# Attention with routed experts on one core: the boundary between early and late tokens moved from 48 to 52 of 64 tiles

## What is computed

```python
x = x + tanh(g_xattn[0]) * attention(layernorm(x), ctx, ctx, Wq, Wk, Wv, Wp, bp)   # 16 heads of 8
x = x + tanh(g_ffn[0]) * experts(layernorm(x), gate, w0, w1, wo)

# experts: 8 of them, hidden size 256, each token goes to two
top_k_weights, top_k_indices = top_k(x @ gate, 2)
p = softmax(top_k_weights)
y = sum over the two chosen n of  p[n] * ((silu(x @ w0[n]) * (x @ w1[n])) @ wo[n])
```

## Time and profile before

| | |
|---|---|
| median of 3 runs | 582.92 us (582.74 to 583.54) |
| the profiled execution, its own time | 583.09 us |
| its span in the trace | 581.3 us |
| outside the span | 1.8 us |
| mean granted TensorE clock | 0.983 |

### The profile page before, as it was taken

The page is one execution under the profiler, slowest core; times in us unless marked ns, Lnnn a source line. Parts: engine busy times, 40 slices in busy tenths (PEclk is TensorE's granted clock), DMA queues, the critical chain, the costliest instruction groups (busy, mean ns, idle before and its releaser), DMA issues.

```text
span 581.3 us, 20236 instructions
## 1 busy us (share of the span) xinstructions
PE 548.9 (94%) x5964; PEld 459.1 (79%) x5965; DVE 405.7 (70%) x1356; ACT 411.7 (71%) x1083; POOL 379.2 (65%) x520
## 2 busy tenths in 40 slices
PE   8999999999999999999999998799999999999960
PEld 6777777777777777777777777699999999999950
DVE  5888988898888888898898875634333333335773
ACT  4788888888888888888898887456566666655640
POOL 3236676767767767767676657777767666766770
PEclk9999999999999999999999999989999999999995
DMA  3742121121221211212212113333323333336997
GB/s 86 219 132 73 49 83 57 53 74 55 61 66 59 77 50 59 77 50 74 67 53 79 40 49 107 133 102 107 104 91 95 91 91 95 94 91 182 324 322 217
DMA packets 70246, 57.96 MB, mean 100 GB/s; under 512 B 8966, under 2 KB 66062, under 8 KB 70192
## 3 DMA queue, kind: packets, MB, share of 16 engines
q1 hardware_dynamic: 52672, 35.98, 21.6%
q0 software_dynamic: 8640, 16.93, 8.7%
q10 hardware_dynamic: 8880, 4.39, 2.6%
HBM read 29.84 MB, written 24.15 MB: 93 GB/s over the span
## 4 chain that ended last, share of the span: by engine, by line
PE 80%; issue 7%; DVE 6%; POOL 3%; DMA 2%; ACT 1%; POOLq 0%; SPq 0%; ACTq 0%; DVEq 0%
PE psH L546 18%; PE psH L460 12%; PE psO L516 8%; PE psH L446 7%; PE psH L452 6%; PE psK L494 5%; PE psO L560 5%; PE psG L560 4%; PE psO L487 3%; PE psO L488 3%; PE psO L476 2%; DVE mx L872 2%; POOL results L1132 2%; PE psX L468 2%; PE psX L498 1%
## 5 line engine op out<-in xcount | busy, mean ns | idle before, releaser
L1132 POOL DMA_INDIRECT results<-ys,zin x142 | 142.0, 1000 | 54.8 <-issue 50.3
L1083 POOL DMA_INDIRECT lists<-zp,dest x128 | 128.2, 1002 | 63.5 <-DVE dest L887 33.6
L546 PE MATMUL psH<-zT,wcur 128*128 128x256 f32 x568 | 135.9, 383 | 0.0
L625 ACT ACTIVATE ex<-psH,rs 128x512 f32<-128x512 f32 x128 | 81.1, 684 | 51.8 <-PE psH L452 51.8
L546 PEld LDWEIGHTS psH<-zT,wcur 128*128 128x128 f32 x568 | 103.3, 192 | 11.3
L992 DVE TENSOR_TENSOR hm<-psH,hs 128x512 f32<-128x512 f32 x71 | 49.1, 692 | 85.9 <-PE psH L546 51.2
L872 DVE TENSOR_REDUCE mx<-psH 128x8 fp32r<-128x512 f32 x128 | 82.5, 686 | 5.0 <-PE psH L446 0.3
L516 PEld LDWEIGHTS psO<-v,pT 128*64 128x64 f32 x2048 | 64.9, 138 | 24.9 <-ACT v L671 23.1
L1114 POOL TENSOR_TENSOR kvr<-ropA,ropB 128x256 f32<-128x256 f32 x64 | 46.5, 727 | 50.4 <-DVE ropB L949 50.0
L460 PE MATMUL psH<-ident,ex 128*128 128x128 f32 x512 | 76.3, 284 | 0.3 <-ACT ex L625 0.2
L516 PE MATMUL psO<-v,pT 128*64 128x64 f32 x2048 | 73.7, 225 | 0.4 <-DVE x1r L940 0.4
(11 more groups left out here) (157 smaller groups left out, 991.5 us busy)
## 6 DMA issues: line engine op xcount, KB each, us to landing
zin<-lists SPq DMA_DIRECT2D x71, 130.0 KB, 2.1
yy<-results SPq DMA_DIRECT2D x16, 512.0 KB, 5.5
xres<-x1r SPq DMA_DIRECT2D x32, 128.0 KB, 2.2
out_dram<-xres ACTq DMA_DIRECT2D x16, 256.0 KB, 4.1
xring<-in_x_dram SPq DMA_DIRECT2D x31, 128.0 KB
cring<-in_ctx_dram SPq DMA_DIRECT2D x31, 128.0 KB
results<-ys,zin POOLq DMA_INDIRECT x142, 2.3
lists<-pad SPq DMA_DIRECT2D x16, 130.0 KB, 2.8
```

Source lines behind the costliest of these rows:

```text
L546: last = pe.matmul(bank[t.buf(2)][:, k * ET:(k + 1) * ET], wcur[:, t.buf(2), a, k * P:(k + 1) * P], zT[:, t.buf(2), :], start=True, stop=True)
L625: nc.scalar.activation(ex[:, t.buf(2), h, :].rearrange("p (g c) -> p g c", g=2), psH[h][:, :, 0:256], ACT.Exp, scale=rs[:, t.buf(4) // 2, ...
L1083: nc.gpsimd.indirect_dma_start(lists, bass.IndirectOffsetOnAxis(ap=dest[:, t.buf(4), j:j + 1], axis=0), zp[:, t.buf(4), j, :], None).then_ ...
L1132: nc.gpsimd.indirect_dma_start(results, bass.IndirectOffsetOnAxis(ap=zin[:, t.buf(8), h, D:D + 1].bitcast(U32), axis=0), ys[:, t.buf(8), h ...
```

## The change

`EARLY` becomes 52 in place of 48. By the formulas of the code `NFULL` becomes 45 in place of 41, `NEARLY` 59 in place of 55 and `CHUNKS_EARLY` 13 in place of 12. `COMBINE_AT` was 60 and is now `NEARLY + 5` = 64. A new constant `CHUNKS_INSIDE` = 72 − 64 = 8 counts the chunks that are summed inside the steps; it was 12 under the old formula. Chunks 8 to 12 are early, but are summed after the last step.

```diff
-EARLY = 3 * NT // 4
+EARLY = 13 * NT // 16
...
-COMBINE_AT = NET + 1 - CHUNKS_EARLY
+COMBINE_AT = NEARLY + 5
+CHUNKS_INSIDE = NET + 1 - COMBINE_AT
...
                 EXPERTS.run(act, experts_step, since=1)
-                for k in range(CHUNKS_EARLY - 1, NCHUNK):
+                for k in range(CHUNKS_INSIDE - 1, NCHUNK):
                     store(k)
...
                 EXPERTS.run(dve, experts_step, since=1)
-                for k in range(CHUNKS_EARLY, NCHUNK):
+                for k in range(CHUNKS_INSIDE, NCHUNK):
                     combine(k)
```

## The result

The changed kernel takes 587.14 us (median of 4 runs, 586.7 to 587.82), against 583.23 us for the kernel before, measured beside it. The ratio is 1.0068, with a 95% interval of 1.0052 to 1.0084. The forecast was 586.5 us and slower.

A forecast was written before the change was run, and what follows sets the result against it. PE bounds the kernel until the last product, then full DMA engines from 549 us to the end: span 581.3 + 3.4 = 584.7, plus 1.8 us outside it, gives 586.5 us; range 583.0 to 589.0 us.

The forecast's parts named there:

- A chunk's sum four steps later, four chunks left at the last product: Sums under the experts: each comes four steps later, leaving four chunks more, 3.15 MB, to move at the last product.
- What the hole takes: DMA engines, 560 to 571 us: room for 1806 + 102 KB of 3146; 1238 KB do not fit, +3.4 us.
- The bounds: Main term at other DMA rates: +5.2 us at 317 GB/s, +2.1 at 390, +0.8 at 435; case 583.7 to 588.6 us.
- The loop: Expert steps: four have no sum in them, so PE wins at most 0.20 us.
- The first table: DVE's attention steps: last three pieces move to steps 58 to 60; taken as zero, bounds −1.5 and +0.3 us.
- The wait at 377 us: Wait of 3.56 us for expert tile 8, hanging on POOL's list of scatters, which the change does not touch.
- The wait for the scatters: Before fetch 13: gate opens at 571.3 to 572.2 instead of 568.5, hidden by about two microseconds of queued bytes.
- The hole did not take everything: Faster rival, last fetches: the hole takes all bytes, only the shorter row of fetches counts, 581.6 us; chance 0.12.
- The late gate: Rival: last scatter's signal waits for queued stores until 575 or later, fetch 13 is late, 588 to 590 us; chance 0.16.
- the two rules of the Trainium skill: DMA: completion signals land after the engine's earlier writes; ceilings of 435 GB/s for the fabric, about 358 for HBM.

The follow-up runs named there:

- the late start alone: Kernel before with sums from expert step 64 instead of 60 and SP's takes in the changed kernel's order; 587.71 us, ratio 1.0067.
- after_again: The changed kernel itself, measured again beside other runs; 587.04 us, ratio 1.0056 to the kernel before.
- no_gate: Changed kernel, but its last three fetches read chunks 0 to 2 and do not wait for the last scatters; 586.4 us, ratio 1.0055.
- sums62: Changed kernel with sums from step 62, first four fetches ahead of tile 67's take, each later take ahead of its fetch; 585.1 us, ratio 1.0023.
- half_after: Changed kernel with each fetch bringing half its bytes, the other half of the buffers zeroed; 582.94 us, ratio 0.9995 to the kernel before.
- eager3: Changed kernel with sums from step 62 and the first three fetches ahead of tile 67's take; 660.5 us on the slower chip, ratio 1.005.
- late_start2: Kernel before with sums from step 64 and SP's takes in the changed kernel's order, on the slower chip; 660.67 us, ratio 1.0076.
- half_before: Kernel before with each fetch bringing half its bytes, the other half of the buffers zeroed; 581.84 us, ratio 0.9975.
- sums58: Kernel before with sums from step 58 instead of 60 and the first three fetches ahead of the takes; 584.08 us, ratio 1.0008.
- e48_eager3: Kernel before with sums from step 58 and the first three fetches ahead of the takes, on the slower chip; ratio 0.9985.

## Why the prediction was right

The mechanism held, and the size came out near: span 584.9 us against 584.7 forecast, 587.14 us against 586.5. That it came out so near is in part luck, since errors of up to 0.9 us in the terms took each other away. By its steps:

- *A chunk's sum four steps later, four chunks left at the last product.* Right. The sum behind the last product (560.12) is chunk 5's, and the late start alone gives the whole loss.
- *What the hole takes.* The stretch grew by 4.1 us, not 3.4, and three terms of that sum were off. The free room was counted at 362 GB/s, but 564 to 571 us moved 338 and 560 to 564 us moved 293, less than the 311 of before. That is 7 × 24 = 168 KB, and 72 + 102 = 174 KB, less than assumed, or +0.9 us at 362 GB/s. The bytes still to move at the last product were counted too high: from its start to the end the profiles show 4.96 MB before (21.3 × 233) and 7.82 MB after (25.39 × 308), which is 2.86 MB more and not 3.15, or −0.8 us. The two were not at the same point: beyond the chunk summed right behind the last product, three fetches were already issued after (chunks 6 to 8), and only two before (chunks 10 and 11), where fetch 12 stood behind the scatters. And the last 4.3 us moved 156 GB/s, not 192, or +0.4 us. With all three the sum is +4.0 us. In the columns of the earlier trace rows, the kernel before and then, in two lines, the kernel after:

```profile
560.00:581.30 21.30, 1.99 (x16) 1.63 (x14) 10.11 (x16) 1.25 (x4) 5.86 (x6) 0.62 0.77 233
```

```profile
559.51:584.90 25.39, 1.99 (x16) 1.63 (x14) 15.55 (x23) 1.25 (x4) 5.90 (x6) 0.61 0.97 308
580.60:584.90 4.30, 0.00 (x0) 0.00 (x0) 1.38 (x2) 0.00 (x0) 0.00 (x0) 0.50 0.53 156
```

- *The bounds.* The forecast counts half of the free room of 560 to 564 us, but the sums for 390 and 435 GB/s count all of it. With half they are +2.5 and +1.3 us in place of +2.1 and +0.8. Neither rate came up.
- *The loop.* I allowed 0.2 us and counted none. The last product is 0.49 us earlier here and 1.07 us earlier in after_again, against 560.00. One profile each can't tell more. The hole's 0.7 us and these 0.5 us nearly cancelled in the forecast of the span, which is luck too.
- *The first table.* Zero was right. Its pieces now slow the steps that end at 338.32 and 344.01 (11.78 us for the two, against 10.51 for the same steps before), and the steps that they left take 10.82 us against 11.98. The last tile's `x1r` starts at 352.59, 0.06 us earlier than before:

```profile
332.23 0.30 DVE L941 TENSOR_TENSOR x1r<-psO,bpg 128x136 f32<-128x136 f32 x1 [0.43 <-PE psO L489]
...
338.32 0.30 DVE L941 TENSOR_TENSOR x1r<-psO,bpg 128x136 f32<-128x136 f32 x1
...
344.01 0.30 DVE L941 TENSOR_TENSOR x1r<-psO,bpg 128x136 f32<-128x136 f32 x1 [0.29 <-PE psO L489]
```

- *The wait at 377 us* stayed: 3.58 us.
- *The wait for the scatters.* Its time was right, its cover was not quite. I put the gate at 571.3 to 572.2; fetch 13 was issued at 571.99, 6.04 us after the start of the last scatter. I called it hidden by about 2 us. By the stretch of no_gate it cost 0.6 to 0.9 us, by the ratios nothing that can be told from none. The backlog I reckoned in bytes covers the engines, but DVE needs chunk 13 itself, and it came 2.98 us after chunk 12: their sums start at 573.82 and 576.80. The last scatter on POOL and the fetch on SP, from their timelines:

```profile
565.95 0.98 POOL L1133 DMA_INDIRECT results<-ys,zin  x1 [0.30 <-issue]
```

```profile
571.99 0.94 SPq L379 DMA_DIRECT2D yy<-results  x2
```

- *The rivals.* The hole did not take everything: that needed 465 GB/s. The late gate was no rival here but the next bound: sums62 and half_after, which take the bytes away, run into it, with the last scatter in the chain that ended last.

On the two rules of the Trainium skill weighed ahead ("DMA: Bandwidth & Descriptors"): the full stretches of after, 338 to 360 GB/s, stay by the lower of the two ceilings; no_gate moved 371 GB/s from 571 to 577 us, a little above it and far from the upper one. The later signal in a full system is seen here: where the last scatter is in the chain that ended last, it lands in 4.85 us (half_after), 5.05 (sums62), 5.07 (eager3) and 5.32 (late_start2) with fetches in flight, and in 2.09 or 2.10 in the hole (before, half_before, sums58, e48_eager3). Which writes the signal waits for, no run shows.

## What to carry to other kernels

When work is moved to a later place so that less of it stands behind a final wait, count the bytes that are unmoved when the last computation ends, before and after, against the room in the idle stretch at the rate of the full stretches. Here four chunks of 0.786 MB met counted room for about two and a half, and the one fetch saved behind the wait was worth less than a microsecond. Count the fetches already under way too, at the same point in both kernels. Filling an idle stretch can also delay the signal that ends it: here that signal took 2.09 us in the hole and about 5 us in the full stretch. And in a queue that waits in order, a transfer that the next step needs must stand ahead of any that waits for a later result.

## What the runs showed of the hardware that I had not expected

- The last scatter took 2.09 us to land with the engines empty and 5.05 us with them full (sums62). I had taken 4.9 from the loaded steps; that this later landing takes back the gain of a filled hole, as in sums62, I had not priced.
- One of the chips ran the unchanged kernel in 656.86 us (23 runs, 653.55 to 663.48) where the others took 583.2 to 583.7 (medians). Its steps are uneven there, with waits of up to 8.0 us (late_start2, on ACT's scalings) that the trace puts down to no engine of the core but calls remote. The cause stays open. This is one of them on DVE among the last expert steps of late_start2, with the releaser in brackets:

```profile
611.66 0.42 DVE L986 COPY zT<-psX 128x256 f32<-128x256 f32 x1 [2.35 <-remote]
```

The stretch behind the last product was the same there within 0.8 us (26.2 and 25.6; 21.7 and 21.3; 22.6 and, in another order of takes, 23.4), so that it could be read across chips where the whole time could not.
